# Scores of the first attention from high and low turned keys side by side: eight products of 256 columns in place of twelve of 128

## The reference, cut to what matters

```python
def _L0_xattn_ref(text, features, Wq_w, Wq_b, Wk_w, Wk_b, fn_w, qn_w, kn_w):
    features_n = rmsnorm(features, fn_w)
    Q = rmsnorm(einsum('btd,fd->btf', text, Wq_w) + Wq_b, qn_w)
    K = rmsnorm(einsum('bsd,fd->bsf', features_n, Wk_w) + Wk_b, kn_w)
    scores = einsum('btf,bsf->bts', Q, K) / sqrt(512)
    return einsum('bts,bsf->btf', softmax(scores), features_n)
x = x + _L0_xattn_ref(_layernorm(x), ctx, ...)   # 32 sequences of 64 rows, width 512
```

## Time and profile before

| what | value |
|---|---|
| median of three runs | 1511.28 us (1510.58 to 1512.31) |
| the profiled execution | 1511.27 us, its span 1509.5 us |
| PE busy | 1463.2 us (97%) |
| DVE, ACT, POOL busy | 1127.8, 795.1, 710.3 us |
| first attention | about the first 176 us |

### The profile page before, as it was taken

How to read it: one execution, slowest core, us unless ns; L and a number is a source line. 1 busy time by engine, 2 the same in 40 slices (tenths; PEclk the granted TensorE clock), 3 DMA queues, 4 the chain that set the end, 5 groups by cost and what they waited for, 6 DMA issues and landing times.

```text
span 1509.5 us, 27579 instructions
## 1 busy us (share of the span) xinstructions
PE 1463.2 (97%) x9895; PEld 846.4 (56%) x9895; DVE 1127.8 (75%) x2172; ACT 795.1 (53%) x3201; POOL 710.3 (47%) x668
## 2 busy tenths in 40 slices
PE   5999999999999799999999999999999999999998
PEld 4888745555555455555555555555565555555554
DVE  5788787878876888776776676677677677667868
ACT  5678841211223576556546654754664565565763
POOL 5668875454565353334334343433434333343553
PEclk9999999999999999999999999999999999999999
DMA  7454435333344565653553554455445445334622
GB/s 248 147 175 136 123 81 126 98 77 50 65 88 72 117 147 84 110 119 64 100 105 53 95 88 81 86 87 95 81 80 105 79 73 103 64 60 67 99 50 112
DMA packets 358936, 146.87 MB, mean 97 GB/s; under 512 B 342304, under 2 KB 342688, under 8 KB 356112
## 3 DMA queue, kind: packets, MB, share of 16 engines
q1 hardware_dynamic: 357504, 137.77, 45.1%
q10 hardware_dynamic: 1296, 7.34, 1.5%
HBM read 58.02 MB, written 4.19 MB: 41 GB/s over the span
## 4 chain that ended last, share of the span: by engine, by line
PE 55%; DVE 5%; ACT 3%; DMA 1%; POOL 1%; issue 1%; SPq 0%; DVEq 0%; POOLq 0%; ACTq 0%
PE bank L72 18%; PE bank L74 17%; PE bank L73 17%; PE bank L2439 3%; ACT a_prob L1836 2%; DMA a_pT_lo<-a_p_lo 1%; POOL a_prob L1707 1%; DVE a_oT_lo L2106 1%; DVE x_res L2193 1%; DVE a_qve L2045 1%; ACT a_oT_lo L1813 0%; DVE a_p_lo L2094 0%; DVE a_nmx L2082 0%; DVE a_qr_lo L2035 0%; POOL a_xr_lo L1731 0%
## 5 line engine op out<-in xcount | busy, mean ns | idle before, releaser
L1836 ACT ACTIVATE a_prob<-a_prob,a_nmx 128x64 f32<-128x64 f32 x512 | 170.2, 334 | 183.7 <-DVE a_nmx L2082 183.7
L72 PE MATMUL bank<-w,a_oT_hi 128*128 128x512 f16 x512 | 194.0, 379 | 1.8 <-DVE a_oT_lo L2106 0.9
L74 PE MATMUL bank<-w,a_oT_hi 128*128 128x512 f16 x512 | 194.0, 379 | 0.0
L73 PE MATMUL bank<-w,a_oT_lo 128*128 128x512 f16 x512 | 194.0, 379 | 0.0
L72 PE MATMUL bank<-w,xT_hi 128*128 128x448 f16 (+1 forms) x512 | 188.0, 367 | 3.1 <-DVE h L1231 2.0
L73 PE MATMUL bank<-w,xT_lo 128*128 128x448 f16 (+1 forms) x512 | 187.7, 367 | 0.0
L74 PE MATMUL bank<-w,xT_hi 128*128 128x448 f16 (+1 forms) x512 | 187.5, 366 | 0.0
L1707 POOL TENSOR_TENSOR a_prob<-a_prob,a_mask 128x512 f32<-128x512 f32 x64 | 79.8, 1268 | 204.5 <-DVE a_prob L2076 204.5
L2031 DVE SCALAR_TENSOR_TENSOR x_res<-bank,a_oinv,x_res 128x512 f32<-128x512 f32 x128 | 95.5, 746 | 75.0 <-PE bank L74 75.0
L1157 ACT CAST f_h_hi<-h 128x448 f16<-128x448 f32 x64 | 35.6, 563 | 209.7 <-DVE h L1231 209.6
L1719 POOL TENSOR_TENSOR a_krs<-a_kve,neg_half 128x4 f32<-128x4 f32 x32 | 32.8, 1026 | 239.6 <-DVE a_kve L2056 239.6
(11 more groups left out here) (351 smaller groups left out, 4120.5 us busy)
## 6 DMA issues: line engine op xcount, KB each, us to landing
shared<-in_l_wq SPq DMA_DIRECT2D x8, 1024.0 KB, 5.0
shared<-in_l_wo SPq DMA_DIRECT2D x8, 1024.0 KB, 5.1
shared<-in_w ACTq DMA_DIRECT2D x8, 896.0 KB, 4.7
craw<-in_w SPq DMA_DIRECT2D x11, 512.0 KB, 3.9
a_wide<-in_l_ctxT SPq DMA_DIRECT2D x16, 256.0 KB, 4.0
x_res<-in_x SPq DMA_DIRECT2D x16, 256.0 KB, 4.5
shared<-in_ctx SPq DMA_DIRECT2D x16, 256.0 KB, 4.4
shared<-in_l_wkv SPq DMA_DIRECT2D x8, 512.0 KB, 3.9
```

What stands on the lines that cost most here:

```text
L72: pe.matmul(out, a_hi, b_hi, start=first, stop=False)
L73: pe.matmul(out, a_lo, b_hi, start=False, stop=False)
L74: return pe.matmul(out, a_hi, b_lo, start=False, stop=last)
L1836: ins = act.activation(pt, pt, ACT.Exp, bias=nmx[:, col:col + 1], accum_out=den[:, col:col + 1])
```

## The change

1. The turned high and low parts of rows, features, queries and keys lay in two blocks (all high parts, then all low parts). They now lie in one block `turned`, the high and the low part of each beside each other; `kT_both` is the 256 columns of both parts of the keys.
2. The scores are eight matmuls: high and low queries as weights, each with the 256 columns of `kT_both` streamed, into 256 columns of `b_s`. The first 128 columns hold the sum with the high keys, the second 128 that with the low keys (the product of low by low comes in as well).
3. VectorE adds the second half in an instruction of its own, between the scaling and the maximum, with a wait of its own on `s_nmx`.
4. The turned probabilities move to columns 256 to 383 of `b_s`; the first two transposed weight maxima go to the bank `b_prep`, the third to the last 128 columns of `b_s`.

```diff
-    b_pT = b_s[:, P:2 * P]
+    b_both, b_pT = b_s[:, 0:2 * P], b_s[:, 2 * P:3 * P]
+    w1_top_T, w2_top_T = b_prep[:, 0:2 * P], b_s[:, 3 * P:4 * P]
...
-    xT4_hi, xT4_lo = (big[:, (4 + h) * KD * D:(5 + h) * KD * D].rearrange("p (k f) -> p k f", k=KD) for h in range(2))
+    turned = big[:, 4 * KD * D:6 * KD * D].rearrange("p (k f) -> p k f", k=KD)
...
-    xT_hi, cT_hi, qT_hi, kT_hi = (xT4_hi[:, :, n * P:(n + 1) * P] for n in range(4))
-    xT_lo, cT_lo, qT_lo, kT_lo = (xT4_lo[:, :, n * P:(n + 1) * P] for n in range(4))
+    xT_hi, cT_hi, qT_hi, kT_hi = (turned[:, :, 2 * n * P:(2 * n + 1) * P] for n in range(4))
+    xT_lo, cT_lo, qT_lo, kT_lo = (turned[:, :, (2 * n + 1) * P:(2 * n + 2) * P] for n in range(4))
+    kT_both = turned[:, :, 6 * P:8 * P]
...
-            act.wait_ge(s_nmx, n * 2 + 2)
+            act.wait_ge(s_nmx, n * 3 + 3)
...
             dve.scalar_tensor_tensor(prob[:, :], b_s[:, 0:P], qrs(n), off[:, :], ALU.mult, ALU.add).then_inc(s_nmx, 1)
-            dve.wait_ge(s_nmx, n * 2 + 1)
+            dve.wait_ge(s_nmx, n * 3 + 1)
+            dve.scalar_tensor_tensor(prob[:, :], b_s[:, P:2 * P], qrs(n), prob[:, :], ALU.mult, ALU.add).then_inc(s_nmx, 1)
+            dve.wait_ge(s_nmx, n * 3 + 2)
             dve.tensor_reduce(nmx[:, :], prob[:, :], AX.X, ALU.max, negate=True).then_inc(s_nmx, 1)
...
             for k in range(KD):
-                ins = split_mm(pe, b_s[:, 0:P], qT_hi[:, k, :], qT_lo[:, k, :], kT_hi[:, k, :], kT_lo[:, k, :],
-                               k == 0, k == KD - 1)
+                pe.matmul(b_both, qT_hi[:, k, :], kT_both[:, k, :], start=k == 0, stop=False)
+                ins = pe.matmul(b_both, qT_lo[:, k, :], kT_both[:, k, :], start=False, stop=k == KD - 1)
```

More of the change, by code:

```diff
@@ L727, in w1_scales @@
             dve.wait_ge(s_wmT, 1)
-            dve.tensor_reduce(w1_top[:, :], b_s[:, 2 * P:4 * P].rearrange("p (w n) -> p w n", w=2), AX.X, ALU.max)\
+            dve.tensor_reduce(w1_top[:, :], w1_top_T.rearrange("p (w n) -> p w n", w=2), AX.X, ALU.max)\
                .then_inc(s_wmx, 1)
@@ L752, in w2_scales @@
             dve.wait_ge(s_wmT, 2)
-            dve.tensor_reduce(w2_top[:, 1:2], b_s[:, 2 * P:3 * P], AX.X, ALU.max).then_inc(s_w2m, 1)
+            dve.tensor_reduce(w2_top[:, 1:2], w2_top_T, AX.X, ALU.max).then_inc(s_w2m, 1)
             dve.wait_ge(s_w2m, NP + 3)
@@ L885, in body @@
                 for w in range(2):
-                    ins = pe.transpose(b_s[:, (2 + w) * P:(3 + w) * P], m.wmax_b[:, w, :], m.ident[:, :])
+                    ins = pe.transpose(w1_top_T[:, w * P:(w + 1) * P], m.wmax_b[:, w, :], m.ident[:, :])
                 ins.then_inc(s_wmT, 1)
@@ L889, in body @@
                 pe.wait_ge(s_w2m, NP + 2)
-                pe.transpose(b_s[:, 2 * P:3 * P], m.wmax_b[:, 0, :], m.ident[:, :]).then_inc(s_wmT, 1)
+                pe.transpose(w2_top_T, m.wmax_b[:, 0, :], m.ident[:, :]).then_inc(s_wmT, 1)
             pe.transpose(b_pT, prob[:, :], m.ident[:, :]).then_inc(s_pT, 1)
```

## The result

The changed kernel took 1515.99 us (median of 6 runs, 1515.08 to 1518.58), the kernel before 1510.93 us (6 runs of the same job, 1508.02 to 1512.31): a ratio of 1.0038, 95% interval 1.0027 to 1.0050. That is slower by 5.1 us, where +1.7 was forecast, and outside the range. The profiled execution of the changed kernel took 1518.58 us, the longest of its runs; where I compare it with the profile of before (span 1516.7 against 1509.5, 7.2 us), 2 us more must be explained than between the medians. Of all the executions in this document two, of 8040 and 5384 us in two experiments, lay far off and are left out of the ratios.

What follows compares the result with a forecast made beforehand. PE, busy for 97% of the span, bounds the kernel, with `k_T` released by DVE in tiles 0 to 13; tile terms 0.12 + 0.33 + 0.38 + 0.51 + 0.38 = +1.7 on 1511.3 give 1513.0 us, range 1510.8 to 1515.6.

Steps and rivals of the forecast that it cites:

- Scores: Scores on PE, each tile: eight products of 256 columns at 0.12 us take 0.97 us, ending 0.32 us earlier.
- Addition: New DVE instruction in each tile: maximum, `scale_keys`, exponential and DVE work behind them come 0.38 us later after scores are taken.
- `k_T` hangs on `scale_keys`: Tiles 0 to 13 of the first attention: DVE's `scale_keys` releases PE's `k_T`, 0.06 to 0.08 us before it begins.
- Rivals 1, 2 and 3: Wide product 0.15 us: +3.3 us, chance 0.16; load not hidden: about +10, 0.03; PE orders `k_T`: 1508.1 us, 0.05.
- The sum over tiles: First attention's 16 tiles: 0.12 + 0.33 + 0.38 + 0.51 + 0.38 = +1.7 us.
- tiles 2 to 4: First attention: DVE can take scores only 0.27 us earlier against the 0.38 addition, so +0.11 us each, +0.33.
- the extra 0.13 for the copy of tile 8: Tile 9: +0.13 us because DVE's L639 in tile 8 now waits for ACT's later copy; +0.51 in all.
- the end: Scores of tile 15 wait for a DVE chain going back to the exponential of tile 14: +0.38 us.
- The zeros of tiles 7, 8 and 10 to 13: Tiles bound by POOL: 0.38 us fits idle time in 7, 8, 10; +0.06 fits margins in 11 to 13; cost 0.
- Rival 4: Tiles 5, 9 and the end: queues have slack and absorb the 0.38 us; +0.5 us, 1511.8 us, chance 0.19.
- Behind the attention nothing absorbs it that I can see ... and PE bounds what follows: Stages behind the first attention: the +1.7 us passes through unchanged, with 0 us added or absorbed.
- a known stretch at 520 us: Between 520 and 530 us, granted clock 0.67: work arriving 1.7 us later is worth up to 1 us either way.

Runs made afterwards that it cites:

- the repeat of before: The kernel before run once more with nothing changed, against the kernel before of the same job: median 1511.74 us, ratio 1.0001 (0.9992 to 1.0009).

## Why the prediction was wrong

- **Scores, right.** 0.95 us instead of 1.29, 0.12 us per product; forecast 0.97. Loading and streaming one after the other would have given 1.8 us. That was by the rule of the Trainium skill, "TensorE: Matmul & The Clock Gate", section "The mechanism", by which a load overlaps running matmuls only when the row group differs; the trace disagrees with it at 256 columns as it did at 512. The same section also lets a load be pulled ahead when it targets the background weight buffer, and with that sentence the 0.12 us agree.
- **Addition, right.** 0.38 to 0.39 us; the maximum 0.78 behind the first addition where 0.76 was forecast.
- **`k_T` hangs on `scale_keys`, right.** It begins 0.06 us behind it in tiles 0 to 13, and the wait is listed now in all 14. Rivals 1, 2 and 3 fell with these three points.
- **The sum over tiles, right in kind and 0.4 us too high.** 1.26 us from tile 2 on against 1.66. Tiles 5 and 6 hit (+0.38, +0.05), tiles 2 to 4 cost 0.06 instead of 0.11, tile 9 0.39 instead of 0.51 (the extra 0.13 for the copy of tile 8 did not come), the end 0.24 instead of 0.38. The zeros of tiles 7, 8 and 10 to 13 held. Rival 4, that queues absorb it, is refuted by tiles 5 and 9.
- **The step that failed** is the sentence "Behind the attention nothing absorbs it that I can see ... and PE bounds what follows", from which I took the 1.7 us through to the end unchanged. It counted only the delay that is handed on. Three terms arose behind it, to which the forecast gave nothing:
  - *The clock:* I widened the range by 1 us for a known stretch at 520 us, and missed that the change lengthens a wait of PE at tile 15, in my own, from 1.37 to 1.81 us. The profiles without a lower clock between 170 and 210 us have 35.7 to 35.8 us for the stage there, those with it at both waits 36.9 to 37.3; in the pair of profiles it is 1.25 us. That the fall goes with the wait is shown by filling it; that the 0.44 us more brought it on is not.
  - *DVE's last block of instructions:* +1.08 us in both profiles of the changed kernel, gone in all three with 16 slots more in DVE's stream; in one of them the rest of layer 2 grew by 0.9 us.
  - *PE's stream, 128 instructions shorter:* +2 us in layer 2, reversed and reproduced by instructions that compute nothing. By what path is open.
- **Whether they account for it all.** Tiles 1.3, end 1.1, PE's stream 2.0 and a clock term between 0 and 1.25 make 4.4 to 5.6; the measured medians differ by 5.1. The profile pair's 7.2 has 1.5 more ahead of tile 2, where the changed kernel's execution first had the full clock at 22.6 us and the kernel before at 14.7. It differs from execution to execution of one kernel (11.8 us in the repeat of before, whose start is 3.6 us shorter), so I do not count it as the change's. The terms are read from single profiles, and that they add up so well is partly luck.

I had written that the instructions saved were 64 products. Their cost in time was worked out; that they and their loads are also 128 places in a stream was not.

## What to carry to other kernels

When a change leaves the later stages untouched and their time still moves, cut both traces at the same instructions and compare the stages before explaining anything in the changed one; then add instructions that compute nothing and see whether the later stage moves back. A forecast to a tenth of a per cent has to allow for that: here some 2 us came with 128 instructions more or fewer, and an edit that wins less than that can only be judged in its own stage. Where an edit lengthens a wait of PE, look at the granted clock behind the wait as well as at the wait; here, filling a wait of 1.81 us with products whose output nobody reads made the stage behind it 1.1 us shorter. And compare a suspected mark with the repeats of the kernel before: a packet more on a queue and an unexplained wait of 0.6 us stood in them too.

## What the runs showed of the hardware that I had not expected

- Instructions come in blocks through DMA queues while the kernel runs: 78 packets of 16 KB for PE, and 58 or 59 of 8 KB on a second queue, whose 0.48 MB fit the other four engines together. In the profiles in which a block of DVE's was fetched 1.8 us behind DVE's last work, the end took 1.0 to 1.1 us longer.
- 128 instructions more or fewer on PE, 0.6% of its stream, moved a stage of 963 us by 1.7 to 2.4 us: adding them shortened it in the kernels with 64 products fewer and lengthened it in the kernel before.
- Waits on a semaphore that is already set took about 0.05 us per instruction on PE (0.4 us for 8).
- POOL's addition of 128 by 128 elements took 0.65 us, half of the 1.30 us of its 512-element rows, not a quarter.
- Behind a PE wait of 1.81 us the granted clock was 0.57 in the window from 176 to 180 us, and 1.00 when transpositions filled the wait. Behind a wait of 1.97 to 1.99 us it fell in 10 of 15 profiles.
